# Four operands of three-pass matmuls as two fp16 parts, before as two fp32r parts

## Chip, cores and metric

The kernel runs on one core of one Trainium2 chip. The metric is the device time of one launch in microseconds, the median of several runs. The engines are TensorE (PE, with its weight loads listed apart as PEld), VectorE (DVE), ScalarE (ACT), GpSimd (POOL) and SyncE (SP), which here only issues DMAs.

## What is computed

One transformer layer in fp32 on 2048 tokens of width 128: a layer norm, causal attention with 16 heads of 64, a residual, a second layer norm, and a feed-forward part with one shared and 8 routed experts, of which each token takes two.

```
x = x + attention(layernorm(x), qkv_w, qkv_b, out_w, out_b)
x = x + ffn(layernorm(x), gate_w, expert_gate, expert_up, expert_down, shared_...)

attention:  qkv = einsum('bse,ehd->bshd', x, qkv_w) + qkv_b;  q, k, v = split(qkv)
            logits = einsum('bqhd,bkhd->bhqk', q, k) / sqrt(64), causal mask
            attn = einsum('bhqk,bkhd->bqhd', softmax(logits), v)
            return einsum('bqhd,hde->bqe', attn, out_w) + out_b
```

The change is in two of these products: the projection to q and k, and the output projection of the attention.

## The kernel before

Five instruction streams are written out by hand, one for each engine, and semaphores tie them. The order on each engine is the order of the code. Matrices are held transposed, 128 features on the partitions and the 2048 tokens (T) along the columns, in 4 blocks (NB) of 512 columns (BLK).

**Split operands.** For accuracy close to fp32, an operand is held as two parts, a rounded high part and a low part that holds the rest, and a product of two such operands is three matmuls into the same PSUM bank: high x high, high x low, low x high. Helper `mm3` issues them, at lines L1198, L1199 and L1200. Its users are the two products below. The high parts are made by a converting copy (of ACT for the weights and the first norm, L705, L709, L646; of DVE for the attention output, L1048), the low parts by a subtraction (of POOL for the weights, L544 and L549; of DVE for the norm, L815, and the attention output, L1050). The parts of q and k, of v, of the probabilities and of the routed experts are fp16 already.

**Prologue** (up to some 47 us): the input is normalised and turned into `xn_hi` and `xn_lo`, the weights of the first pair of heads are split, and the four blocks of q and k of head 0 are projected.

**Heads** (some 47 to 720 us): for each of 16 heads PE walks through 20 slots, one for each pair of key tiles of a block of queries (`GROUPS`; block b has 2(b+1) of them). A slot holds the scores (`scores`, L1308 and L1309, two fp16 matmuls for each of two key tiles, up to 512 columns), a causal mask (L1321), and the product of probabilities and v of the slot three before (`p_times_v`, L1340, L1342, L1344: short fp16 matmuls of 64 or 65 columns). ACT takes two exponentials of each slot's scores (L719, L720), POOL subtracts them for the low part of the probabilities (L585).

Between them stand background tasks, which use three PSUM banks (`bg`) in turn: PE writes one, DVE drains it. Their slots are fixed by tables (`V_SLOTS`, `ATT_SLOTS`, `ATT_LAST`) and by a planner that spreads the maxima. They are:

- `qk`, for the next head, in slots 0 to 3: `mm3` of `w_hi`, `w_lo` with `xn_hi`, `xn_lo`, 512 columns; DVE drains it in L1007 and L1009 (ACT's L674 for head 0). SP's queue then copies the parts from one set of partitions to another (L434, L440, L447), and PE waits for them before the first maximum of each four tiles;
- `max`, in slots 4 to 17 or so: the scores once more (L1233, fp16), of which DVE takes row maxima (L1024 with the mask, L1028 without), then `shift` (L1238);
- `v`, two for each head (L1223, plain fp32);
- `att_t` and `att_y`, for a finished pair of heads, in slots 6/8, 10/12, 16/18 of the odd head and 4/6 of the next even one: four transposes (L1243), DVE's split into `att_hi` and `att_lo` (L1048, L1050), then `mm3` of `wo_hi`, `wo_lo` with these, and DVE adds the bank to the residual (L1053). The last pair doesn't use `mm3` but one fp32 matmul (L1249).

So `mm3` is issued 64 times for q and k (4 of them in the prologue) and 28 times for the output.

**The rest** (from some 720 us): second norm, routing, shared expert, a scatter of rows, 39 tiles of the routed experts and the sum of all. No operand of it is among those that change.

## Time and profile before

| | us |
|---|---|
| median of 3 runs | 928.4 |
| lowest and highest run | 926.62, 929.88 |
| the profiled execution, its own time | 927.27 |
| its span in the trace | 925.5 |
| PE, DVE, ACT, POOL busy | 862.5, 696.2, 685.6, 712.2 |
| mean granted TensorE clock, of full speed | 0.979 |

How to read it: the span runs from the first to the last instruction of the program, 1.8 us less than the execution's own time. An engine's busy time is the union of its instructions' times. Matmuls overlap in it: each row of a matmul holds also the time in which its results leave the array, so that what a matmul costs the next one is read from start to start.

### The profile page before, as it was taken

What the parts mean: (1) busy time and instruction counts of PE and PEld (TensorE: products, weight loads), DVE (VectorE), ACT (ScalarE), POOL (GpSimd) and SP (SyncE); (2) the same over time, 40 slices, a digit from 0 to 9 for tenths busy, and PEclk for the clock granted to TensorE, in tenths of its full rate; (3) what the DMA queues carried; (4) which work ended last, traced back from release to release, by engine and by line L of the source; (5) the groups of instructions that cost most, each with busy time, mean ns of one, the idle gap of its engine ahead of it and who ended that gap; (6) DMA issues with size and microseconds to landing.
All of it is one profiled execution on the core that took longest, in us unless ns stands there. A gap on an engine that the chain in (4) does not pass through costs nothing.

```text
span 925.5 us, 25699 instructions
## 1 busy us (share of the span) xinstructions
PE 862.5 (93%) x10266; PEld 595.1 (64%) x10266; DVE 696.2 (75%) x1771; ACT 685.6 (74%) x842; POOL 712.2 (77%) x448
## 2 busy tenths in 40 slices
PE   4788999999999999999999999999999798859996
PEld 3455667666666666666666676666666564438886
DVE  7798797888879797978797979796978356535445
ACT  4456788988898888888988898888889963114442
POOL 1466889998899889988988898888889967344442
PEclk9799999999999999999999999999999999879999
DMA  5121232323232424232301020202020001112214
GB/s 179 24 66 50 56 67 64 67 56 67 63 71 52 75 56 81 59 73 67 66 21 39 19 48 1 57 1 47 2 47 2 2 1 38 46 35 68 61 46 144
DMA packets 60149, 48.33 MB, mean 52 GB/s; under 512 B 8688, under 2 KB 57714, under 8 KB 59904
## 3 DMA queue, kind: packets, MB, share of 16 engines
q1 hardware_dynamic: 57760, 42.48, 20.3%
q0 software_dynamic: 2272, 4.22, 1.3%
q8 instruction: 83, 1.36, 0.6%
q14 instruction: 34, 0.28, 0.1%
HBM read 13.93 MB, written 16.29 MB: 33 GB/s over the span
## 4 chain that ended last, share of the span: by engine, by line
PE 61%; DVE 24%; issue 4%; POOL 4%; ACT 3%; DMA 2%; another core or an unknown queue 1%; SPq 0%; POOLq 0%; DVEq 0%; ACTq 0%
DVE row_max L1028 10%; PE st L1308 7%; PE st L1309 7%; PE bg L1233 6%; PE pv L1340 5%; PE pv L1342 4%; PE pv L1344 4%; POOL p_parts L585 4%; DVE junk L1024 3%; PE bg L1223 3%; PE bg L1483 3%; PE bg L1198 3%; PE bg L1199 2%; PE bg L1200 2%; DVE att_parts L1050 2%
## 5 line engine op out<-in xcount | busy, mean ns | idle before, releaser
L585 POOL TENSOR_TENSOR p_parts<-prob,p_parts 128x1024 f16<-128x1024 f32 x320 | 613.2, 1938 | 101.1 <-ACT p_parts L720 99.0
L719 ACT ACTIVATE prob<-st,p_bias 128x1024 f32<-128x1024 f32 x320 | 330.9, 1034 | 110.5 <-PE st L1309 78.6
L720 ACT ACTIVATE p_parts<-st,p_bias 128x1024 f16<-128x1024 f32 x320 | 330.3, 1032 | 0.0
L1028 DVE TENSOR_REDUCE row_max<-bg 128x1 f32<-128x512 f32 x384 | 250.5, 684 | 8.4 <-PE bg L1233 7.1
L1340 PE MATMUL pv<-v_parts,p_parts 128*128 128x65 f16 x2176 | 232.7, 193 | 3.1 <-POOL p_parts L585 2.6
L1342 PE MATMUL pv<-v_parts,p_parts 128*128 128x64 f16 x2176 | 233.0, 195 | 0.0
L1344 PE MATMUL pv<-v_parts,p_parts 128*128 128x65 f16 x2176 | 232.0, 192 | 0.0
L1308 PE MATMUL st<-qk_parts 128*128 128x512 f16 (+3 forms) x640 | 222.2, 350 | 5.8 <-ACT p_parts L720 3.5
L1340 PEld LDWEIGHTS pv<-v_parts,p_parts 128*128 128x128 f16 x2176 | 202.3, 96 | 28.0 <-DVE attn L1080 8.8
L1309 PE MATMUL st<-qk_parts 66*128 66x512 f16 (+3 forms) x640 | 220.3, 350 | 0.0
L1233 PE MATMUL bg<-qk_parts 128*128 128x512 f16 (+3 forms) x640 | 210.7, 352 | 9.5 <-DVE row_max L1028 2.2
L1342 PEld LDWEIGHTS pv<-v_parts,p_parts 128*128 128x128 f16 x2176 | 201.8, 97 | 16.0 <-issue 0.3
L1344 PEld LDWEIGHTS pv<-v_parts,p_parts 128*128 128x128 f16 x2176 | 202.2, 99 | 0.0
L1024 DVE CUSTOM_DVE_ANT_0 junk<-bg,mask_wide 128x128 bf16<-128x128 f32 (+3 forms) x256 | 121.5, 482 | 3.0 <-PE bg L1233 2.0
L1233 PEld LDWEIGHTS bg<-qk_parts 128*128 128x128 f16 x640 | 62.9, 98 | 76.1 <-DVE row_max L1028 13.2
L1308 PEld LDWEIGHTS st<-qk_parts 128*128 128x128 f16 x640 | 62.7, 98 | 61.5 <-issue 22.5
L1309 PEld LDWEIGHTS st<-qk_parts 66*128 66x128 f16 x640 | 62.6, 98 | 42.5 <-issue 1.1
L1007 DVE TENSOR_SCALAR qk_parts<-bg,qk_bias 128x512 f16<-128x512 f32 x60 | 44.9, 748 | 59.7 <-PE bg L1200 59.7
L622 POOL DMA_INDIRECT y_dram<-p_parts,v_parts x39 | 37.8, 969 | 50.0 <-DVE p_parts L1159 37.4
L777 ACT ACTIVATE prob<-st 128x352 f32<-128x352 f32 x39 | 18.1, 463 | 51.0 <-PE st L1464 41.3
L1167 DVE TENSOR_TENSOR prob<-prob,st 128x352 f32<-128x352 f32 x39 | 20.3, 521 | 46.1 <-issue 40.4
L1009 DVE SCALAR_TENSOR_TENSOR qk_parts<-bg,qk_bias,qk_parts 128x512 f16<-128x512 f32 x64 | 47.9, 751 | 3.4 <-ACT qk_parts L674 1.3
(230 smaller groups left out, 1086.5 us busy)
## 6 DMA issues: line engine op xcount, KB each, us to landing
qk_parts<-qk_parts SPq DMA_DIRECT2D x192, 64.0 KB, 2.0
row_dram<-fill SPq DMA_DIRECT2D x8, 1290.0 KB, 10.3
qk_parts<-qk_parts SPq DMA_DIRECT2D x16, 256.0 KB, 3.0
stage_raw<-ffn_w SPq DMA_DIRECT2D x16, 176.0 KB, 2.6
v_parts<-row_dram SPq DMA_DIRECT2D x39, 64.5 KB
qk_parts<-y_dram SPq DMA_DIRECT2D x8, 256.0 KB, 4.7
w_raw<-qkv_w SPq DMA_DIRECT2D x8, 192.0 KB, 2.3
down_w<-ffn_w SPq DMA_DIRECT2D x1, 1536.0 KB, 8.2
```

What stands on the lines that cost most here:

```text
L585: nc.gpsimd.tensor_tensor(o, a, b, ALU.subtract).then_inc(p_lo_ready, 1)
L719: nc.scalar.activation(o32, src, ACT.Exp, bias=p_bias[:], scale=D ** -0.5)
L720: nc.scalar.activation(o16, src, ACT.Exp, bias=p_bias[:], scale=D ** -0.5).then_inc(exp_done, 1)
L1009: nc.vector.scalar_tensor_tensor(out=q_lo_shift[s][:, blk(b)], in0=bank, scalar=bias, in1=k_lohi[s][:, blk(b)], op0=ALU.add, op1=ALU.subtr ...
L1024: nc.vector.tensor_tensor_reduce(masked[k % BGRING][:, 0:width], bank[:, 0:width], mask_wide[:, BLK - width:BLK], 1.0, -3.0e38, ALU.add, A ...
L1028: nc.vector.tensor_reduce(row_max[:, t, c:c + 1], bank, AX_X, ALU.max).then_inc(bg_drained, 1)
L1233: mm = nc.tensor.matmul(bank[:, 0:width], q_hihi[s][:, tile(t)], k_lohi[s][:, c * BLK:c * BLK + width], start=True, stop=True)
L1308: nc.tensor.matmul(out, k_lohi[s][:, tile(kt)], q_hihi[s][:, q], start=True, stop=False)
L1309: mm = nc.tensor.matmul(out, k_hi_one[s][0:D + 2, tile(kt)], q_lo_shift[s][0:D + 2, q], start=False, stop=not diagonal)
L1340: nc.tensor.matmul(out, p_hi[:, n % PRING, cols], v[:, 0:D + 1], start=(kt == 0 and j == 0), stop=False, skip_group_check=True)
L1342: nc.tensor.matmul(out[:, 0:D], p_hi[:, n % PRING, cols], v[:, D + 1:VW], start=False, stop=False, skip_group_check=True)
L1344: mm = nc.tensor.matmul(out, p_lo[:, n % PRING, cols], v[:, 0:D + 1], start=False, stop=(kt == 4 * b + j), skip_group_check=True)
```

## The change

The types of four groups of buffers change from fp32r (4 bytes) to fp16 (2 bytes): `xn_hi` and `xn_lo` (the normalised input), `split`, which holds `w_hi`, `w_lo` (projection weights) and `wo_hi`, `wo_lo` (output weights), and `att_parts`, which holds `att_hi` and `att_lo`. The streams are not touched: every engine has the same instructions in the same order before and after, with other types of operands. The buffers become smaller, by 8 KB for each partition for the normalised input, 3 KB for `split`, 2 KB for `att_parts`, and what is allocated behind them moves by that.

```diff
-F32, F32R = mybir.dt.float32, mybir.dt.float32r
+F32 = mybir.dt.float32
...
-        att_parts = sb("att_parts", [P, 2 * BLK], F32R)
+        att_parts = sb("att_parts", [P, 2 * BLK], F16)
...
-        xn_hi = sb("xn_hi", [P, T], F32R)
-        xn_lo = sb("xn_lo", [P, T], F32R)
+        xn_hi = sb("xn_hi", [P, T], F16)
+        xn_lo = sb("xn_lo", [P, T], F16)
...
-        split = sb("split", [P, 12, P], F32R)
+        split = sb("split", [P, 12, P], F16)
```

## Rows read from the trace of the kernel before

**Rows 1.** The page: span, then busy us and share of each engine.
```profile
span 925.5 us, 25699 instructions
...
PE 862.5 (93%) x10266; PEld 595.1 (64%) x10266; DVE 696.2 (75%) x1771; ACT 685.6 (74%) x842; POOL 712.2 (77%) x448
```

**Rows 2.** The page: chain that ended last, by engine, then by line.
```profile
PE 61%; DVE 24%; issue 4%; POOL 4%; ACT 3%; DMA 2%; another core or an unknown queue 1%; SPq 0%; POOLq 0%; DVEq 0%; ACTq 0%
DVE row_max L1028 10%; PE st L1308 7%; PE st L1309 7%; PE bg L1233 6%; PE pv L1340 5%; PE pv L1342 4%; PE pv L1344 4%; POOL p_parts L585 4%; DVE junk L1024 3%; PE bg L1223 3%; PE bg L1483 3%; PE bg L1198 3%; PE bg L1199 2%; PE bg L1200 2%; DVE att_parts L1050 2%
```

**Rows 3.** Busy us of a steady stretch: PE, PEld, DVE, ACT, POOL; clock, DMA share, GB/s.
```profile
260.00:360.00 100.00, 99.08 (x1318) 67.68 (x1317) 83.06 (x192) 87.68 (x97) 90.77 (x52) 1.00 0.37 72
```

**Rows 4.** Weight loads: L1198 (ns: min/median/max), L1233 (busy us, mean ns, idle before).
```profile
L1198 PEld LDWEIGHTS bg<-xn_hi,split x64: 186/188/338, 12.1 to 683.1; 128*128 128x128 f32 x64
...
L1233 PEld LDWEIGHTS bg<-qk_parts 128*128 128x128 f16 x640 | 62.9, 98 | 76.1 <-DVE row_max L1028 13.2
```

**Rows 5.** PE in order of time (start us, duration us): an output projection, fp32r.
```profile
301.34 0.19 PE L1344 MATMUL pv<-v_parts,p_parts 128*128 128x65 f16 x1
301.36 0.48 PE L1198 MATMUL bg<-att_parts,split 128*128 128x512 f32 x1
301.68 0.40 PE L1199 MATMUL bg<-att_parts,split 128*128 128x512 f32 x1
...
302.15 0.39 PE L1308 MATMUL st<-qk_parts 128*128 128x512 f16 x1
302.38 0.38 PE L1309 MATMUL st<-qk_parts 66*128 66x512 f16 x1
```

**Rows 6.** PE in order of time: as many columns, all fp16.
```profile
304.85 0.20 PE L1344 MATMUL pv<-v_parts,p_parts 128*128 128x65 f16 x1
304.88 0.38 PE L1233 MATMUL bg<-qk_parts 128*128 128x512 f16 x1
...
305.75 0.38 PE L1308 MATMUL st<-qk_parts 128*128 128x512 f16 x1
```

**Rows 7.** PE in order of time: slot 18, from ahead of L1198 to behind it.
```profile
138.38 0.38 PE L1309 MATMUL st<-qk_parts 66*128 66x512 f16 x1
...
139.46 0.33 PE L1309 MATMUL st<-qk_parts 66*128 66x384 f16 x1
```

**Rows 8.** PE in order of time: the first projection of the prologue.
```profile
12.14 0.78 PE L1198 MATMUL bg<-xn_hi,split 128*128 128x512 f32 x1
12.71 0.63 PE L1199 MATMUL bg<-xn_lo,split 128*128 128x512 f32 x1
13.14 0.63 PE L1200 MATMUL bg<-xn_hi,split 128*128 128x512 f32 x1
```

**Rows 9.** Waits: who waited for whom, us in total, times, longest.
```profile
DVE qk_parts L1007 <- PE bg L1200: 59.7, 44, 3.7
...
DVE res L1053 <- PE bg L1200: 9.0, 22, 0.7
```

**Rows 10.** In order of time, with the idle time before: POOL, then DVE.
```profile
175.03 6.32 POOL L585 TENSOR_TENSOR p_parts<-prob,p_parts 128x1024 f16<-128x1024 f32 x3 [0.94 <-ACT p_parts L720]
...
264.14 2.13 POOL L585 TENSOR_TENSOR p_parts<-prob,p_parts 128x1024 f16<-128x1024 f32 x1 [0.94 <-ACT p_parts L720]
...
239.99 0.69 DVE L1048 CAST att_parts<-bg 128x512 fp32r<-128x512 f32 x1 [0.42 <-PE bg L1243]
```

**Rows 11.** Pieces of the chain in order of time: start us, us, what.
```profile
370.57 2.92 DMA qk_parts<-qk_parts
...
637.37 3.81 DMA qk_parts<-qk_parts
```

**Rows 12.** Groups by line and shape: busy us, mean ns, idle before.
```profile
L1016 DVE CAST v_parts<-bg 128x512 f16<-128x512 f32 x28 | 19.4, 692 | 13.4 <-PE bg L1223 13.2
...
L1048 DVE CAST att_parts<-bg 128x512 fp32r<-128x512 f32 x28 | 19.3, 690 | 3.2 <-PE bg L1243 2.9
...
L544 POOL TENSOR_TENSOR split<-w_raw,split 128x256 fp32r<-128x256 f32 x8 | 5.8, 725 | 5.5 <-ACT split L705 5.5
```

## The prediction

> **What bounds the kernel now.** I read the totals first: one core, a profiled execution of 927.27 us with a span of 925.5 us, PE busy 93% of it and no other engine above 77% [rows 1]. A busy PE says little here, since a matmul row of 0.38 us is followed by the next one after 0.22 us, so I went on to the chain of waits. It gives PE 61% and DVE 24% [rows 2], and it names all three lines of the group of three matmuls that the change touches: L1198 with 3%, L1199 and L1200 with 2% each. The 92 groups of three take about 0.79 us each (301.36 to 302.15 from start to start [rows 5]), 72.7 us or 7.9% of the span; the chain's 3 + 2 + 2% is rounded, and nearly all of that is on the path. Following the chain in order of time, I find 86 of the 92 on it. The six that are not start at 12.1, 17.3, 48.5, 61.0, 369.5 and 636.3 us.
>
> In a stretch of the steady heads PE is busy 99.1 of 100 us at the full clock, POOL 90.8, ACT 87.7, DVE 83.1 [rows 3]. So TensorE sets the pace, with short stretches in which DVE (the row maxima) or POOL (the low parts of the probabilities) ends last.
>
> **The change, part by part.** No instruction is added, dropped or moved on any engine. Four kinds of buffers change type: the normalised input, the split projection weights, the split output weights and the split attention output.
>
> *Weight loads and matmuls.* A stationary part in fp32r loads in 188 ns, one in fp16 (L1233, same 128x128) in 98 ns [rows 4]. What counts is start to start. One group of today: from L1344 at 301.34, the last matmul ahead of it, to L1309 at 302.38 are 1.04 us, for one short matmul and four of 512 columns [rows 5]. The same row of sizes all in fp16: L1344 at 304.85, then L1233 at 304.88, L1308, L1309, L1233 and again L1308 at 305.75, that is 0.90 us, 0.22 for each of 512 columns [rows 6]. The first interval of the fp32r group is 0.32 against 0.22 us (a long load cannot hide behind a 65-column matmul that is over in 0.03 us), the next two are 0.47 together against 0.44, and the fp16 matmul behind the group has 0.23 against 0.22. Difference: **0.14 us for each group**. The streaming rate itself is nearly the same in both types, so this is all that there is.
>
> How many: 64 groups are projections (16 heads, 4 blocks), 28 are output projections (7 pairs, 4 blocks). 81 of them follow a short L1344. 7, those of slot 18, follow L1309 with 512 columns, and there the load is mostly hidden: 138.38 to 139.46 is 1.08 us today [rows 7], against four intervals of 0.22 and one of 384 columns at 0.17, 1.05; gain about 0.04. The 4 of the prologue run at a lower clock: 0.57 us for the first interval, 0.43 for the second [rows 8], gain 0.14 as well.
>
> On the path lie 77 of the 81 (77 x 0.14 = 10.8 us), all 7 (0.3 us) and 2 of the prologue (0.3 us): 11.4 us.
>
> *What is late next.* A shorter group only pays until another engine ends last. Behind the projections DVE stands idle for the result: 44 waits of L1007 on L1200, 59.7 us, 1.4 us each; behind the output projections 22 waits of L1053, 9.0 us, 0.41 us each [rows 9]. All that is well over 0.14. The 16 groups of slot 3 have no such wait, since DVE normalises there, but its next wait on PE comes soon behind and is again longer than 0.14 (0.42 us at 239.99 [rows 10]). POOL's long stretches at the ends of the early even heads start with a wait, too: 0.94 us at 175.03 [rows 10], so they start earlier as PE does. POOL is idle 9.2 us of 100 [rows 3], and a pair of heads (89.1 us from 175.03 to 264.14) wants only 11 x 0.14 = 1.5 us.
>
> One cover is gone already: q and k parts go by SP's queue from one set of partitions to another, and slot 4 needs them. At 370.57 such a copy takes 2.92 us to land and the row maxima of slot 4 wait for it [rows 11]. It is issued behind the group of slot 2 or its drain, so what the group of slot 3 saves is lost there. Two such places are the groups at 369.5 and 636.3, which I have left out already; I charge two more of the fourteen steady heads with the same, by choice, since PE now comes to slot 4 a little earlier against the copy: 2 x 0.14 = 0.3 us back.
>
> *Writing and splitting the parts.* DVE's cast into fp32r takes 690 ns (L1048), its cast of the same size into fp16 takes 692 ns (L1016) [rows 12]: nothing. The low part is a subtraction with a PSUM operand in both, at the same pace. POOL's subtraction for the weights (L544) takes 725 ns for 256 elements, 8 times [rows 12]; no row shows that size in fp16, so I bound it by the same row from both sides, half of it or twice: 8 x 0.36 = 2.9 us of POOL's work less, or 5.8 us more, on an engine with 9 us in 100 to spare. In the whole of the time I take zero, with POOL's stretch at the end of a head (rival B) as the place where more would show. ACT's copies into fp16 are not on the path in the steady heads. The DMAs are the same, the four buffers are never a source or a target of one.
>
> Sum: 11.4 - 0.3 = **11.1 us** less, 927.27 - 11.1 = 916.2 us against the profiled execution. The median of the runs shown, 928.4, lies 1.1 us above that execution, so I forecast **917.3 us**.
>
> The Trainium skill speaks against the larger part of this. Its page "TensorE: Matmul & The Clock Gate", section "Weight-path perf modes", says of 8-bit operands that a weight load scales with the number of columns, not with bytes; the same section also says that a fast load applies to 128 weights of any type but FP32. By the first sentence the load would stay as long as it is; by the second it gets shorter. The trace sides with the second for fp16 against fp32r (98 and 188 ns), and I follow the trace.
>
> **The rivals.**
>
> *A, forecast.* 9.5 to 12.5 us less, 916 to 919.
>
> *B, another engine swallows part of it.* The place would be POOL's stretches at the ends of four even heads, where the 5 groups of such a head would then give nothing (4 x 5 x 0.14 = 2.8 us), and the SP copies ahead of slot 4 in all heads from 2 on (12 more groups, 1.7 us). Together 11.1 - 4.5 = 6.6 us less, 921.8. For it: POOL at 90.8% and two copies that bind today. Against it: the waits of rows 9 and 10, which are all longer than the gain.
>
> *C, the load does not get shorter*, so the change does not do what it should. Then the first interval stays at 0.32 and only the small terms are left: (0.47 - 0.44) + (0.23 - 0.22), some 0.04 us for each of the 86 groups, 3.4 us less, 925.0. For it: today's fp16 loads are all of other buffers. Against it: the load of L1233 takes 98 ns whatever stands ahead of it, and in [rows 6] it follows a short matmul without a delay. This is also what the skill's sentence on columns would give.
>
> *D, slower.* The copies of the q and k parts collide with other transfers or with each other. Their landing today takes 2.0 us in the median and 2.92 and 3.81 us in the two places where they bind [rows 11]. If PE's earlier arrival at slot 4 meets copies that land as late as 3.81 us in each of the 14 steady heads, each head pays up to 1.8 us, less the margin that it has. It decides from 11.1 / 14 = 0.8 us a head; at 1.0 us a head the change ends at 928.4 + 2.9 = 931.3. For it: those two places, without a plain reason for the slow landing. Against it: size, number and order of the copies stay, and their source, DVE's drain of the group, moves forward with PE, so the margin shrinks by one group's 0.14 us at most.
>
> **How the numbers follow.** A 0.76, B 0.11, C 0.05, D 0.04, and 0.04 for what I have not seen. Most likely 917.3. The range: below, all 92 groups on the path give 12.9 us (915.5), and a quick chip some 1.5 us more, as the runs shown spread from 926.6 to 929.9; so 914.2. Above, it takes B in: 922.0. Outside lie C, D and the unseen, and the edges. A measurement of this kernel tells some 0.3% (2.8 us) from no change. A, B and C are faster by more than that, C only just, so faster 0.90, within 0.3% 0.05, slower 0.05.
>
> **What the changed profile would show.** L1198 to L1200 as f16, with a load of 98 ns; L1344 to L1309 across a group 0.90 us in place of 1.04; 64 us in place of 73 for the 92 groups; the pair of heads, 89.1 us long (175.03 to 264.14 for the same POOL stretch), shorter by 1.5 us; DVE's waits for L1200 shorter in sum, not gone. L1048, L1050 as long as now. If B holds, the groups are shorter and the waits of POOL's or DVE's successors on PE grow: PE idle before L1340 for POOL, or before L1233 for a DMA. If C holds, the load row reads 188 ns in fp16. The forecast is wrong if the intervals shrink but the pair of heads does not, or if the tail behind 720 us, which holds none of the groups, changes length by more than 1 us.

## Result and the profile after

| us | before | after |
|---|---|---|
| median of 4 runs each (lowest to highest) | 928.47 (926.62 to 929.88) | 919.51 (917.31 to 920.30) |
| ratio, with 95% interval | | 0.990 (0.988 to 0.992) |
| profiled execution, its span | 927.27, 925.5 | 918.86, 917.1 |
| mean granted TensorE clock, of full speed | 0.979 | 0.974 |

The change makes the kernel 9.0 us faster; 11.1 were forecast, and the time lies 2.2 us above the forecast of 917.3 and inside its range. A second pair, with more runs of each (below), gives 10.5 us. The direction, the place and the mechanism of the forecast held. What was off are small terms: the loss to late copies was sized too small, the prologue gave nothing, and the part behind the last group, taken as fixed, came out 2 us longer in both pairs of profiles.

The page of the kernel after: span, busy times, and the chain that ended last, by engine and by line (answers to [rows 1, 2]):

```profile
span 917.1 us, 25699 instructions
...
PE 853.2 (93%) x10266; PEld 577.4 (63%) x10266; DVE 695.6 (76%) x1771; ACT 684.9 (75%) x842; POOL 710.7 (77%) x448
...
PE 60%; DVE 25%; issue 5%; POOL 4%; ACT 3%; DMA 2%; SPq 1%; POOLq 0%; DVEq 0%; ACTq 0%
DVE row_max L1028 10%; PE st L1308 7%; PE st L1309 7%; PE bg L1233 7%; PE pv L1340 5%; PE pv L1342 4%; PE pv L1344 4%; POOL p_parts L585 4%; DVE junk L1024 3%; PE bg L1483 3%; PE bg L1223 3%; PE bg L1200 2%; PE bg L1198 2%; PE bg L1199 2%; DVE att_parts L1050 2%
```

The instructions are as many as before, PE's busy time falls by 9.3 us, and L1198 goes from 3% to 2% of the chain. VectorE, ScalarE and GpSimd keep their busy times to 1.5 us.

The weight loads of L1198 after (ns: min/median/max, as in [rows 4]):

```profile
L1198 PEld LDWEIGHTS bg<-xn_hi,split x64: 95/96/151, 12.1 to 672.9; 128*128 128x128 f16 x64
```

PE in order of time, an output projection after (start us, duration us), the counterpart of [rows 5]:

```profile
297.92 0.19 PE L1344 MATMUL pv<-v_parts,p_parts 128*128 128x65 f16 x1
297.95 0.38 PE L1198 MATMUL bg<-att_parts,split 128*128 128x512 f16 x1
298.16 0.38 PE L1199 MATMUL bg<-att_parts,split 128*128 128x512 f16 x1
298.38 0.38 PE L1200 MATMUL bg<-att_parts,split 128*128 128x512 f16 x1
298.60 0.38 PE L1308 MATMUL st<-qk_parts 128*128 128x512 f16 x1
298.81 0.38 PE L1309 MATMUL st<-qk_parts 66*128 66x512 f16 x1
```

The load is 96 ns where it was 188. From L1344 to L1309 are now 0.89 us, where [rows 5] had 1.04, and every interval is 0.21 or 0.22, the first one too. Over the 81 groups behind a short L1344 the median is 892 ns, and it was 1039 ns before. Taken apart by the width of the L1308 that follows, the difference is 0.150 us for 66 of them and 0.147 us for the other 15; I use **0.148 us for each group**.

The steady stretch after, columns as in [rows 3]:

```profile
260.00:360.00 100.00, 98.75 (x1348) 66.36 (x1346) 81.81 (x191) 90.15 (x101) 92.17 (x53) 1.00 0.35 66
```

TensorE is as full as before, and ScalarE and GpSimd are 2.5 and 1.4 points busier, since their work comes in less time. TensorE still sets the pace.

Waits after (who waited for whom: us in total, times, longest), against [rows 9]:

```profile
DVE qk_parts L1007 <- PE bg L1200: 53.6, 43, 3.5
...
DVE res L1053 <- PE bg L1200: 6.7, 22, 0.6
```

In order of time, GpSimd and then VectorE, against [rows 10]:

```profile
173.92 2.13 POOL L585 TENSOR_TENSOR p_parts<-prob,p_parts 128x1024 f16<-128x1024 f32 x1 [0.94 <-ACT p_parts L720]
...
261.42 2.13 POOL L585 TENSOR_TENSOR p_parts<-prob,p_parts 128x1024 f16<-128x1024 f32 x1 [0.94 <-ACT p_parts L720]
...
237.41 0.69 DVE L1048 CAST att_parts<-bg 128x512 f16<-128x512 f32 x1 [0.25 <-PE bg L1243]
```

Groups after, against [rows 12], the second one by its line alone (ns: min/median/max):

```profile
L1048 DVE CAST att_parts<-bg 128x512 f16<-128x512 f32 x28 | 19.3, 690 | 2.0 <-PE bg L1243 1.8
...
L544 POOL TENSOR_TENSOR split<-w_raw,split x8: 667/671/686, 9.2 to 594.6; 128x256 f16<-128x256 f32 x8
```

VectorE's waits for the group became shorter and did not go, so VectorE did not become what ends last behind these groups. The pair of heads between the two stretches of GpSimd takes 87.50 us, and it took 89.11: 1.6 us less, 1.5 were forecast. GpSimd still begins its long stretch behind the same wait of 0.94 us. The cast takes 690 ns in both types, and GpSimd's subtraction 671 ns against 725.

### The profile page after: what moved, and what is told of

Its sections match the earlier page's. It is cut to its first block, busy times and chain, and to the rows that moved or that the text cites. A ratio compares the mean times of both kernels' runs of the same rounds, so it can differ in the third digit from the quotient of the medians.

```text
span 917.1 us, 25699 instructions
## 1 busy us (share of the span) xinstructions
PE 853.2 (93%) x10266; PEld 577.4 (63%) x10266; DVE 695.6 (76%) x1771; ACT 684.9 (75%) x842; POOL 710.7 (77%) x448
## 4 chain that ended last, share of the span: by engine, by line
PE 60%; DVE 25%; issue 5%; POOL 4%; ACT 3%; DMA 2%; SPq 1%; POOLq 0%; DVEq 0%; ACTq 0%
DVE row_max L1028 10%; PE st L1308 7%; PE st L1309 7%; PE bg L1233 7%; PE pv L1340 5%; PE pv L1342 4%; PE pv L1344 4%; POOL p_parts L585 4%; DVE junk L1024 3%; PE bg L1483 3%; PE bg L1223 3%; PE bg L1200 2%; PE bg L1198 2%; PE bg L1199 2%; DVE att_parts L1050 2%
## 5 line engine op out<-in xcount | busy, mean ns | idle before, releaser
L585 POOL TENSOR_TENSOR p_parts<-prob,p_parts 128x1024 f16<-128x1024 f32 x320 | 612.4, 1935 | 93.5 <-ACT p_parts L720 91.6
L1340 PE MATMUL pv<-v_parts,p_parts 128*128 128x65 f16 x2176 | 232.7, 193 | 3.2 <-POOL p_parts L585 2.6
L1344 PE MATMUL pv<-v_parts,p_parts 128*128 128x65 f16 x2176 | 231.9, 192 | 0.0
L1308 PE MATMUL st<-qk_parts 128*128 128x512 f16 (+3 forms) x640 | 221.7, 349 | 7.4 <-ACT p_parts L720 4.6
L1309 PE MATMUL st<-qk_parts 66*128 66x512 f16 (+3 forms) x640 | 220.6, 351 | 0.0
L1340 PEld LDWEIGHTS pv<-v_parts,p_parts 128*128 128x128 f16 x2176 | 202.3, 96 | 28.4 <-DVE attn L1080 9.0
L1233 PE MATMUL bg<-qk_parts 128*128 128x512 f16 (+3 forms) x640 | 210.7, 353 | 9.8 <-DVE row_max L1028 2.1
L1344 PEld LDWEIGHTS pv<-v_parts,p_parts 128*128 128x128 f16 x2176 | 202.2, 99 | 0.0
L1024 DVE CUSTOM_DVE_ANT_0 junk<-bg,mask_wide 128x128 bf16<-128x128 f32 (+3 forms) x256 | 121.7, 483 | 3.1 <-PE bg L1233 2.1
L1233 PEld LDWEIGHTS bg<-qk_parts 128*128 128x128 f16 x640 | 62.9, 98 | 77.4 <-DVE row_max L1028 13.1
L1309 PEld LDWEIGHTS st<-qk_parts 66*128 66x128 f16 x640 | 62.4, 97 | 52.6 <-issue 1.4
L1308 PEld LDWEIGHTS st<-qk_parts 128*128 128x128 f16 x640 | 62.9, 98 | 50.0 <-ACT p_parts L720 7.0
L1007 DVE TENSOR_SCALAR qk_parts<-bg,qk_bias 128x512 f16<-128x512 f32 x60 | 44.9, 749 | 53.8 <-PE bg L1200 53.6
```

What stands on the lines that cost most here:

```text
L585: nc.gpsimd.tensor_tensor(o, a, b, ALU.subtract).then_inc(p_lo_ready, 1)
L1024: nc.vector.tensor_tensor_reduce(masked[k % BGRING][:, 0:width], bank[:, 0:width], mask_wide[:, BLK - width:BLK], 1.0, -3.0e38, ALU.add, A ...
L1233: mm = nc.tensor.matmul(bank[:, 0:width], q_hihi[s][:, tile(t)], k_lohi[s][:, c * BLK:c * BLK + width], start=True, stop=True)
L1308: nc.tensor.matmul(out, k_lohi[s][:, tile(kt)], q_hihi[s][:, q], start=True, stop=False)
L1309: mm = nc.tensor.matmul(out, k_hi_one[s][0:D + 2, tile(kt)], q_lo_shift[s][0:D + 2, q], start=False, stop=not diagonal)
L1340: nc.tensor.matmul(out, p_hi[:, n % PRING, cols], v[:, 0:D + 1], start=(kt == 0 and j == 0), stop=False, skip_group_check=True)
```

## The experiments

To compare parts of a run, I cut it at the starts of the `shift` drain (L1040), one for each head: h to h+1 is the stretch between those of heads h and h+1. The drain for head h comes in slot 18 of head h-1, so that h to h+1 is in the main the time of head h. Head 15 itself comes behind its drain; the last scores of the kernel before (L1308) start at 764.2 us and the last L1340 at 769.1, so the heads end near 770 us and not near 720, as I had put it at the start. In the table "once more" are repeats of the unchanged kernels; stretches that repeat a pattern are left out.

| us | before once more | after once more | q, k only | output only | 4 matmuls | 2 matmuls |
|---|---|---|---|---|---|---|
| 1 to 2 | 45.77 | 45.20 | 45.02 | 44.98 | 45.54 | 44.54 |
| 2 to 3 | 43.42 | 42.64 | 42.84 | 43.22 | 44.76 | 41.37 |
| 3 to 4 | 45.67 | 44.85 | 45.14 | 45.38 | 46.08 | 44.26 |
| 6 to 7 | 43.43 | 42.63 | 42.84 | 43.21 | 43.93 | 41.37 |
| 7 to 8 | 45.68 | 45.32 | 46.24 | 45.79 | 46.08 | 44.11 |
| 9 to 10 | 45.68 | 45.10 | 45.42 | 45.50 | 46.07 | 44.24 |
| 10 to 11 | 43.43 | 42.63 | 42.84 | 43.24 | 43.94 | 41.37 |
| 13 to 14 | 45.89 | 45.46 | 45.19 | 45.54 | 45.40 | 43.97 |
| start of head 15's | 713.94 | 703.42 | 706.25 | 712.12 | 720.06 | 692.21 |

A stretch that starts with an even head is called short here (43.4 us before), one that starts with an odd head long (45.7 us). The expectations below go by the head at the end of a stretch: their odd stretches are the short ones, their even ones the long ones. The three chips on which the experiments ran give the kernel before other times (929.0, 908.8 and 908.5 us; the last section comes to that), so each is compared on its own chip.

### Both kernels once more, and one half of the change at a time

My theory: the whole gain is the weight load, so it splits by the number of groups, 64 for q and k, 28 for the output. The rival was that something else in one of the two halves carries it, or takes it back.

> The kernel before once more, unchanged. It gives a second profile of it. The changed kernel gained 8.4 us of span in the first pair of profiles: 10.05 us up to the start of the last pair's output projection (L1249), of which 1.0 us had been given back in head 0, and then 1.7 us given back behind it, where none of the changed matmuls is. Theory (the granted clock of TensorE, at its low level in other places of the prologue and of the routing from one execution to the next, by chance): this second profile differs from the first by 0.5 to 2.5 us in the stretches 0 to 60 us and 770 to 830 us, by less than 0.5 us in the heads 2 to 15 altogether apart from a single hiccup, and its ratio is 1.000 within 0.002. Rival (the faster heads shift the phase in the same way each time): the second profile of before shows its low clock in the same places as the first, to 0.3 us.

> The changed kernel once more, unchanged. Clock by chance: its stretches 0 to 60 us and 770 us to the end differ from those of the first profile of it by 0.5 to 2.5 us, and the 13 stretches from head to head (h2 to h15) are the same within 0.1 us each. Ratio to before 0.988 to 0.991 (9 to 11 us less). Rival (the losses outside the heads belong to the change): head 0 costs 1.0 us more than before again, and the tail 1.7 us more.

The first half alone has `xn_hi`, `xn_lo` and the projection weights in fp16:

```diff
-        split = sb("split", [P, 12, P], F32R)
+        split = sb("split", [P, 8, P], F16)
+        wo_split = sb("wo_split", [P, 4, P], F32R)
```

> Only the normalised input and the projection weights are fp16; the output weights, in a tensor of their own, and the attention output stay fp32r. 64 of the 92 groups are fast. A group counts at its measured 0.148 us: 60 groups in the heads x 0.148 = 8.9 us, less some 1.5 us for those of slot 3 or of head 0 that are not on the path: 7.4 us less, ratio 0.992, and 4 x 0.148 = 0.6 us less for each head. If the output projections were what counted (rival): under 3 us.

The second half alone has `att_parts` and the output weights in fp16:

```diff
-        split = sb("split", [P, 12, P], F32R)
+        split = sb("split", [P, 8, P], F32R)
+        wo_split = sb("wo_split", [P, 4, P], F16)
```

> Only the attention output and the output weights are fp16; projections stay fp32r. 28 groups: 21 x 0.148 + 7 x 0.05 = 3.5 us less, ratio 0.9963, and together with the kernel with only the projections in fp16 the same as the whole change within 1 us. If gains of the two kinds cover each other (rival), the sum of both alone is 1.5 us or more above the whole.

| | median us | ratio to before, 95% | gain us |
|---|---|---|---|
| before once more | 929.05 | 1.000 (0.998 to 1.002) | 0.0 |
| after once more | 918.54 | 0.989 (0.987 to 0.991) | 10.5 |
| q and k only | 921.59 | 0.993 (0.990 to 0.995) | 7.4 |
| output only | 925.54 | 0.996 (0.995 to 0.998) | 3.5 |

The two halves give 10.9 together, the whole 10.5. The profiles agree: from the start of head 1's drain to head 15's the whole saves 9.9 us, the first half 6.8 and the second 3.5.

Of the two repeats, the kernel before took the same time again, and its clock fell in other places (its low stretch in the prologue began at 29.8 us, not at 30.6), as I had expected. Of the changed kernel two expectations failed. Four of the stretches, not none, differ from the first profile by more than 0.1 us: 1 to 2 by 0.40, 7 to 8 by 0.23, 9 to 10 by 0.32, 13 to 14 by 0.26. And the loss in the tail came again, as the rival said: behind head 15's drain the two profiles of before take 209.98 and 211.22 us, the two of after 212.03 and 213.09. The loss in head 0 did not come again.

How the gain splits over single stretches shows in the starts of the `shift` drain, heads 9 to 11. The rows give ns (min/median/max of the drain), then first and last start in us. Before once more:

```profile
L1040 DVE SCALAR_TENSOR_TENSOR shift_row<-bg,shift_row x3: 278/278/279, 405.4 to 494.5; 16x128 f16<-16x128 f32 x3
```

After once more:

```profile
L1040 DVE SCALAR_TENSOR_TENSOR shift_row<-bg,shift_row x3: 278/278/278, 399.9 to 487.7; 16x128 f16<-16x128 f32 x3
```

With q and k alone (one more line stands above it, so that it is L1041 here and in the next):

```profile
L1041 DVE SCALAR_TENSOR_TENSOR shift_row<-bg,shift_row x3: 278/278/279, 401.6 to 489.8; 16x128 f16<-16x128 f32 x3
```

With the output alone:

```profile
L1041 DVE SCALAR_TENSOR_TENSOR shift_row<-bg,shift_row x3: 278/278/278, 405.2 to 494.0; 16x128 f16<-16x128 f32 x3
```

First to last start is 89.1, 87.8, 88.2 and 88.8 us. In the table, a short stretch has five groups behind a short matmul and one of slot 18: 5 x 0.148 + 0.06 = 0.80 us (0.06 is the difference of the medians over the 7 groups of slot 18, 1.087 and 1.028), and 43.43 - 42.63 is 0.80. With q and k alone it is four groups, 0.59, measured 0.59; with the output alone 0.148 + 0.06 = 0.21, measured 0.20 (0.19 to 0.22). In a long stretch the six groups should give 0.89, and give 0.82 where nothing else happens (3 to 4); with the output alone it is 0.30 there, as two groups should, with q and k alone 0.53, not 0.59, so the missing 0.07 belongs to q and k. One stretch went the wrong way: 7 to 8 takes 46.24 us with q and k alone, 0.56 more than before, since a copy comes late there (below). So the shorter groups explain the short stretches to 0.01 us, the long ones to 0.07 us. The rival falls: neither half carries the gain alone, and neither takes it back.

### Is it the load that stood out? A longer matmul ahead of it

A 188 ns load can hide behind a matmul of 512 columns (0.22 us), but not behind one of 65. If the gain is the exposed load, it must shrink when the background task stands behind a score pair. If fp32r matmuls themselves were the slow part, it would stay.

```diff
-                    first, second_at = (0, 0) if h == H - 1 else (1, 2)
+                    first, second_at = (0, 0) if h == H - 1 else (0, 1)
```

In the new order, with the types of before and with those of after:

> The kernel before with the first background task of each slot of heads 0 to 14 issued on TensorE behind the slot's first pair of score matmuls, not ahead of it. The fp32r groups of slots 0 to 3 then follow an L1309 of 128 to 512 columns, no longer a 65-column L1344. Theory (0.10 of the 0.148 us is a weight load that a short matmul cannot hide): groups behind a 512-column matmul cost as those of slot 18 do, 0.05 us more than fp16; the span from the matmul ahead of the group to the one behind is 0.05 us over the fp16 kernel with the same order. So this order narrows the gap between the two types from 0.80 us to 0.3 us a head. What the new order does by itself, to both kernels, I can't tell: between 5 us less and 10 us more, since scores come earlier and the maxima later. Rival (the first interval is long for another reason, a change of type from fp16 to fp32r): the gap stays at 0.8 us a head.

> The same new order in the changed kernel. Theory of the hidden load: it is only 3 to 6 us faster than the kernel before in the same order (10.5 us in the old order). Rival: 9 to 11 us faster.

Measured: 942.65 us (ratio 1.036, 1.034 to 1.038) and 938.00 (1.032, 1.030 to 1.035) against 908.83 for the kernel before on that chip. Between them are 4.65 us, where the old order has 10.5 on the first chip and 11.7 on the third. PE in order of time, in the new order with the types of before:

```profile
382.68 0.38 PE L1309 MATMUL st<-qk_parts 66*128 66x512 f16 x1
382.71 0.58 PE L1198 MATMUL bg<-xn_hi,split 128*128 128x512 f32 x1
383.13 0.40 PE L1199 MATMUL bg<-xn_lo,split 128*128 128x512 f32 x1
383.37 0.40 PE L1200 MATMUL bg<-xn_hi,split 128*128 128x512 f32 x1
383.60 0.34 PE L1308 MATMUL st<-qk_parts 128*128 128x384 f16 x1
```

The same with the types of after:

```profile
382.24 0.38 PE L1309 MATMUL st<-qk_parts 66*128 66x512 f16 x1
382.45 0.38 PE L1198 MATMUL bg<-xn_hi,split 128*128 128x512 f16 x1
...
383.10 0.38 PE L1308 MATMUL st<-qk_parts 128*128 128x512 f16 x1
```

From L1309 to L1308 are 0.92 and 0.86 us. The same step, from the matmul ahead of the group to the first one behind it, has these medians: 922 and 868 ns over the 66 groups behind 512 columns, 815 and 762 ns over the 15 behind 256 columns, 867 and 813 ns over the 7 behind 384; behind the 65 columns of the old order it is 814 and 676 ns. So the difference of types is 0.054 us in all 88 groups of the new order and was 0.138. Some 0.08 us of a group was the load that stood out behind the short matmul, and it is hidden behind 256 columns already. The rest stays with fp32r: 0.054 us in this step, mostly in the intervals of 0.24 and 0.23 against 0.22, and 0.065 with the next matmul, 88 x 0.065 = 5.7 us in all, of which 4.65 reach the end. The theory holds: the change from fp16 to fp32r between L1309 and L1198 is there in the new order too, so it isn't what made the first interval long. The new order by itself is far worse, by 34 us with the types of before, where I had expected at most 10: PE is busy only 96.5 of 100 us between 260 and 360 us and waits for ScalarE (1.16 us ahead of the L1308 at 382.47). I did not follow that further.

### One matmul less and one more in each group

How much of a shorter group reaches the end? Two kernels of after's types change the group by a whole matmul of 0.216 us, 92 x 0.216 = 19.9 us of PE's time. The first leaves out L1199:

```diff
-                nc.tensor.matmul(out, w_hi_ap, x_lo_ap, start=False, stop=False, skip_group_check=skip)
```

> The changed kernel without the second matmul of each group of three (high weights by the low part of the moving operand, L1199): 92 fp16 matmuls of 512 columns less, 0.216 us each, so TensorE has 19.9 us less work. It tells how much more there is before another engine ends last. Theory (each stretch has the covers seen in the waits: DVE 0.36 us ahead of L1007 in slot 2, none in slot 3, 0.3 us ahead of L1053, and the copies of slots 3 and 4): the first 0.15 us of a group paid nearly in full, the next 0.22 pays in part: odd stretches 42.63 to 41.8, all in all 12 to 16 us less than the changed kernel. Rival (TensorE alone bounds): 18 to 19 us less.

The second adds low x low:

```diff
+                nc.tensor.matmul(out, w_lo_ap, x_lo_ap, start=False, stop=False, skip_group_check=skip)
```

> The changed kernel with a fourth matmul in each group (low weights by low moving part, which the sum of two parts would need in full): 92 fp16 matmuls of 512 columns more, 0.216 us each. It asks the same as the kernel with two matmuls from the other side. There TensorE's 0.216 us a group came back in full in the odd stretches (42.63 to 41.37) and by half or less in the even ones. Theory (going up, TensorE is what ends last, more and more): odd stretches 42.63 + 6 x 0.216 = 43.93 us, even ones 44.86 + 1.30 = 46.16, together 17 to 20 us slower than the changed kernel. Rival (covers work both ways, half of it hides in waits for DVE): 8 to 12 us slower.

With four the time is 913.07 us (before on that chip 908.49, ratio 1.005, 1.003 to 1.007), 16.3 more than after there (896.82, below), where 17 to 20 were expected. With two it is 885.58 (before 908.83, ratio 0.974, 0.972 to 0.976), 11.2 less than after, where 12 to 16 were expected. Both lie just outside, on the side of less effect. After itself did not run on the chip of the kernel with two, so I use 896.82 of the other quick chip, where before takes 0.3 us less. (The starts of head 15's drain give the same: 720.06, 703.55 and 692.21 us, steps of 16.5 and 11.3.)

| step | PE work us | time us | passed through |
|---|---|---|---|
| four matmuls to three | 19.9 | 16.3 | 82% |
| fp32r to fp16, three matmuls | 13.0 (12.4 in the heads, 4 x 0.148 in the prologue) | 10.5 | 81% |
| three matmuls to two | 19.9 | 11.2 | 57% |

Most short stretches give a whole matmul for each of their six groups both ways (43.94 to 42.63, 41.37; 6 x 0.216 = 1.30). With four matmuls 2 to 3 (44.76) and 12 to 13 (44.31) are longer than that. With two matmuls three short stretches fall short: 4 to 5 takes 43.03 and 8 to 9 takes 42.06, and 14 to 15 takes 40.68 where after has 40.86. The other four take 41.37. In the long ones TensorE's wait for GpSimd (L585) grows from 0.25 to some 0.54 us in 3 to 4, 5 to 6, 7 to 8 and 9 to 10, and copies bind in five stretches. So a shorter group paid less the second time than the first. The steady stretch with two matmuls, columns as in [rows 3]:

```profile
260.00:360.00 100.00, 98.15 (x1368) 66.38 (x1367) 82.79 (x190) 91.24 (x103) 95.03 (x55) 1.00 0.30 63
```

GpSimd is at 95% there.

### Copies that land late

In the long stretches 1 to 2, 7 to 8, 9 to 10 and 13 to 14 the gain is 0.57, 0.36, 0.58 and 0.43 us instead of 0.82, together 1.34 us less. In the first two TensorE waits for a copy of the parts of q and k. Pieces of the chain in order of time in after (start us, us, what):

```profile
363.88 0.76 DVE qk_parts L1007
...
364.66 0.54 SPq L434
...
365.24 0.60 SPq L434
...
365.94 3.22 DMA qk_parts<-qk_parts
...
369.30 0.38 PE bg L1233
```

The copy of the second block for head 8 lands after 3.22 us, where the median of all is 2.0, and PE waits for it. In 9 to 10 the view names another wait of PE (L1233 on `row_max` L1024, 0.51 us at 457.33), but that task waits for the same kind of copy too, and one (L440) landed at 457.20: it was issued late, behind copies that took 2.5 to 3.1 us.

In 13 to 14 it is a copy of another kind. SP in order of time, then PE, in after:

```profile
619.42 1.18 SPq L471 DMA_DIRECT2D qk_parts<-shift_row  x2
...
623.07 0.38 PE L1308 MATMUL st<-qk_parts 128*128 128x512 f16 x1 [0.93 <-issue]
```

The first L1308 of a head waits in the code for the two 4 KB copies of `shift_row` (L1299), whose landing the profile doesn't hold, so the view can name nothing. Their packets tell: they end 1.77 us after the second issue here (at 620.01), and after 1.40 us in most heads.

Why do some land late? I counted over the 208 copies of q and k in the trace of after: of the 62 that take over 2.3 us, 50 have a packet of one of the two queues that the profile calls instruction (q8 and q14) in their time, of the 146 quick ones 20. In before it is 47 of 59 and 17 of 149. Sixteen of the 62 are the 256 KB copies (L447), which take 3.0 us in the median and never under 2.9; without them it is 41 of 46 in after and 37 of 43 in before. That is a correlation; the cause wants a run. I take these queues to bring the engines' code, q8 in 83 packets of 16 KB over the span; no row says what is in a packet. Two rivals: that the collision depends on how many instructions PE has behind it (then extra matmuls in the prologue move it to other heads), or that it is the addresses of the smaller buffers.

> The changed kernel with 64 small matmuls (128x32, ident by ident, into the bank that the attention uses later) at the start of TensorE's stream, where it waits some 9 us for the first norm. They cost no time there but move all later instructions of TensorE by 128 places. In the profiles of the changed kernel the copies of q and k of heads 2, 8, 10 and 14 land in 2.5 to 3.6 us where 1.9 to 2.0 is usual, each time beside one of the 16 KB transfers of the instruction queue, which come every 10 us or so, and heads 7 and 9 (in which the copies for 8 and 10 are made) save 0.3 to 0.5 us where head 11 saves 0.8. Theory (these transfers delay the copies, and at a fixed place of the program): the stretches from head to head that are slow move to other heads: 7 to 8 or 9 to 10 falls to 44.9 us from 45.3 to 45.5, and some other even stretch (5 to 6, 11 to 12, 3 to 4) rises by 0.3 us or more. Total within 1.5 us of the changed kernel. Rival (something else of heads 7 and 9, such as the fills of row_dram): the stretches stay as they are, to 0.1 us.

```diff
+            for _ in range(64):
+                nc.tensor.matmul(pv[:, 0:32], ident[:], ident[:, 0:32], start=True, stop=True)
```

This one, with the lines ahead of the first transposes of the prologue, was built badly. `ident` is fp32, and each such matmul stands as two rows. The group of the added line in its trace (busy us, mean ns | idle before):

```profile
L1351 PE MATMUL pv<-ident 128*128 128x32 f32 x128 | 27.5, 401 | 1.6 <-POOL ident L524 1.6
```

There are 255 instructions more, and the instruction queue has 84 packets in place of 83. If those 255 fill nearly one packet, the pattern was moved round by a whole period. The time is 915.96 us (ratio 1.007, 1.006 to 1.009), with the 27 us of work partly beside the start; the long stretches 7 to 8 and 9 to 10 stay as in after, 45.74 and 45.40 against 45.55 and 45.42. By the letter of the expectation the rival had this run (and the total missed its 1.5 us by far). But if it was moved by a whole period, both rivals say the same here. So again with fp16 operands, 64 loads and 64 matmuls in the same place, ahead of the first transposes of the prologue, together with after unchanged and with after whose buffers are padded to the old addresses:

> The changed kernel once more, unchanged, as the reference beside the next three and as a pair with the kernel before on this chip. The kernel before took 909 us on the chip of the last four runs and 929 us on the first, with the difference in the routing and the first expert tiles (some 760 to 820 us), where none of the changed matmuls is. Theory (the gain is made in the heads, so it is the same number of microseconds on any chip): 9 to 11.5 us less than before, odd stretches from head to head 42.63 us and even ones 44.86, to 0.03.

The extra matmuls with fp16 operands:

```diff
+            ident_h = ident[:].bitcast(F16)
+            for _ in range(64):
+                nc.tensor.matmul(pv[:, 0:32], ident_h[:, 0:P], ident_h[:, 0:32], start=True, stop=True)
```

> The changed kernel with 64 fp16 matmuls (the bits of ident read as fp16, 32 columns) at the start of TensorE's stream. The last try put in 64 fp32 matmuls, each of which ran as two with two loads: 255 instructions, almost exactly one 16 KB transfer of the instruction queue, so that these transfers stood in the same places of the program, and the slow stretches with them; and they took 27 us, 19 of them on the path. These are 128 instructions, half a transfer, and some 0.11 us each, 7 us, inside TensorE's 9 us of waiting. Theory (instruction transfers delay the copies of q and k): the stretches 7 to 8 (45.3 to 45.7 us so far) and 9 to 10 (45.1 to 45.4) come down to 44.9, the transfers now fall in the middle between the old places, and other stretches may rise by 0.3 to 0.5. Rival (something else of these heads): 7 to 8 and 9 to 10 stay above 45.2. Total within 1.5 us of the changed kernel.

The padding:

```diff
         att_parts = sb("att_parts", [P, 2 * BLK], F16)
+        sb("pad0", [P, 2 * BLK], F16)
...
         xn_hi = sb("xn_hi", [P, T], F16)
+        sb("pad1", [P, T], F16)
         xn_lo = sb("xn_lo", [P, T], F16)
+        sb("pad2", [P, T], F16)
...
         split = sb("split", [P, 12, P], F16)
+        sb("pad3", [P, 12, P], F16)
```

> The changed kernel with unused buffers behind the four changed ones, so that every buffer lies at its old address. Theory (types alone matter): same as the changed kernel, ratio to it 1.000 within 0.0015, stretches the same to 0.03 us. Rival (part of the gain is from where the buffers lie): more than 1.5 us slower.

| us | after, third time | extra matmuls | padded |
|---|---|---|---|
| median | 896.82 | 898.76 | 898.17 |
| ratio to before, 95% | 0.989 (0.985 to 0.992) | 0.989 (0.987 to 0.991) | 0.988 (0.986 to 0.990) |
| 1 to 2 | 45.38 | 44.11 | 45.47 |
| 3 to 4 | 44.87 | 45.27 | 44.86 |
| 5 to 6 | 44.88 | 45.14 | 44.87 |
| 6 to 7 | 43.03 | 43.32 | 42.63 |
| 7 to 8 | 45.61 | 44.87 | 45.27 |
| 9 to 10 | 44.99 | 44.88 | 45.39 |
| 11 to 12 | 44.20 | 44.70 | 44.20 |
| 13 to 14 | 45.21 | 44.22 | 44.84 |

After for the third time gains 11.7 us against before on that chip, just over the 9 to 11.5 expected; 1 to 2, 6 to 7, 7 to 8, 9 to 10, 11 to 12 and 13 to 14 are not the 42.63 or 44.86 forecast. With the extra matmuls the loss moves: 1 to 2, 7 to 8 and 13 to 14 fall by 0.7 to 1.3 us, 3 to 4, 5 to 6, 6 to 7 and 11 to 12 rise by 0.3 to 0.5. The two that the theory named, 7 to 8 and 9 to 10, take 44.87 and 44.88 where 44.9 was forecast, though 9 to 10 stood at 44.99 already. With the padding the loss stays in 1 to 2, 7 to 8 and 9 to 10, 13 to 14 is 0.4 lower, and none of the four others rises. Its median is 1.35 us higher, close to the 1.5 at which the addresses would have counted, but that is no loss in the heads: from head 0's last drain (L1040; L1044 here) to head 15's it takes 638.2 us against 638.8, and its low clock in the prologue lasts 3.4 us longer. So I find no effect of the addresses, and one of the number of instructions ahead. The queues in the time of that copy, in after, 365.9 to 369.2 us (packets, MB, share of 16 engines):

```profile
q1 hardware_dynamic: 343, 0.29, 36.8%
q8 instruction: 1, 0.02, 2.2%
```

and with the extra matmuls, 364.8 to 366.8 us, where the view has no row of an instruction queue:

```profile
q1 hardware_dynamic: 258, 0.22, 44.9%
```

There the same copy lands after 1.94 us (issued at 364.82, landed at 366.76), and the chain has no DMA in it (start us, us, what):

```profile
366.80 0.17 PE st L1309
366.97 0.18 PE bg L1233
367.17 0.56 DVE junk L1024
```

The other stretches fit, in this one profile. In 13 to 14 the packets of `shift_row` now end after 1.40 us, and the wait of 0.9 us ahead of L1308 is gone. In 3 to 4 and 6 to 7, which rose, they end after 1.95 and 2.16 us, each time with a 16 KB packet of q8 beside them, and L1308 waits 0.33 and 0.53 us. In 5 to 6 and 11 to 12 two copies of q and k have such a packet beside them (2.7 to 3.0 us), push the next ones back, and L1233 waits 0.41 and 0.47 us.

This shows, by a change that leaves the heads as they are and puts 128 instructions of TensorE, 2 us of work, into the wait at the start, that the transfers of the instruction queue decide in which heads PE waits, and that with one a copy can land more than 1 us later. Moving them does not make a faster kernel: head 15's drain starts at 703.55 us without and 702.27 with the extra matmuls, and the medians, 896.82 and 898.76, lie within each other's spread (1.9 us apart, where at most 1.5 was expected). Of the kernels that form the full sum of three matmuls, none beats after measurably.

## Why the prediction was right, and where it was off

The chain, the count and the mechanism were right, and the time lies in the range. It lies 2.2 us above the most likely value. The two "once more" traces allow an account of the 10.5 us up to head 15's drain (713.94 - 703.42):

| term | forecast us | measured us |
|---|---|---|
| 81 groups behind a short matmul | 81 x 0.14 = 11.3 | 81 x 0.148 = 12.0 |
| 7 groups of slot 18 | 0.3 | 7 x 0.06 = 0.4 |
| prologue, up to the third start of L1040 | 0.3 | -0.2 |
| what groups of the heads do not give (forecast: 4 off the path, 2 behind copies) | -0.8 | -2.2 |
| 0 to 1, which holds no group | 0 | 0.5 |
| sum | 11.1 | 10.5 |

**The rate.** The 0.14 us was read as 1.04 - 0.90 from two single places with two decimals. Over all groups it is 0.148. That is 0.7 us of gain that I had not counted. A median would have been the better row.

**Hidden loads in slot 18.** 0.04 forecast, 0.06 measured (1.03 against 1.09 us), and the new order gives 0.065 for 88 groups.

**The copies are the mis-sized term.** The step "I charge two more of the fourteen steady heads with the same, by choice" was wrong in two ways. It took the loss for one group's 0.14 us at a place, but a stretch in which a copy binds loses 0.24 to 0.46 us. And it took the two places of [rows 11] for fixed ones, while they wander with the transfers of the instruction queue. Four stretches lose 1.34 us, 0.39 of them (13 to 14) by the copies of `shift_row`, for which the forecast had no term. The seven long ones lose 0.07 each besides (0.5 together, a cause that I did not find), and the four groups of head 0, ahead of 0 to 1, give 0.28 of 0.59 us: 2.2 in all. Against it the forecast charged 0.84. This is rival B's copy half, with 1.3 of its 1.7 us, of which some 0.9 by copies of q and k. Its other half, GpSimd at the ends of even heads, does not show: the pair of heads gives 1.6 us. With groups shorter still it would show, as the kernel with two matmuls tells.

**The start.** The prologue has 0.3 us in the forecast and -0.2 in this pair; from one execution to the next it varies more than that (the third start of L1040 is at 46.88 and 46.26 us in the two traces of before). Against it stands 0.5 us that belongs to no group: in 0 to 1 PE waits 0.85 us for a copy of `shift_row` in place of 1.39. In the first pair it was 1.56 in place of 1.34, and with the types of after it is 0.85 or 0.86 in four of the later profiles; why the copy comes earlier there is open. That the sum comes so close to 11.1 owes something to this term, which the forecast did not have: that part is luck.

**Marks.** The load of 98 ns (96), 0.90 us for a group (0.89), the 1.5 us of a pair of heads (1.6), and the waits all came. The lower end of the range has a slip: 915.5 - 1.5 is 914.0, not 914.2. One mark had a slip of the pen: 92 groups would fall from 73 to 72.7 - 92 x 0.14 = 59.8 us, not 64; measured are 0.65 from L1198 to L1308 (297.95 to 298.60), so 60. Another mark failed by its own words: the end behind head 15's drain, without any of the groups, grew from 209.98 to 212.03 us, over the 1 us that I had set. In the second pair it grew again, from 211.22 to 213.09, and the halves have 212.91 and 213.53. So on this chip both pairs of profiles give back some 2 us there, and the spans differ by 8.4 and 8.7 us where the heads had won 10.4 and 10.5. The forecast had nothing for it. It is not the types by themselves: on the quick chips, where the stands of TensorE told of in the last section are missing, the end takes 191.79 us with the types of before (in the new order) and 191.26 with those of after. On the first chip the clock is at its lower level for 20.5 us between 770 and 835 us in both traces of before, and for 24 to 27 us in the four with fp16 parts; why it falls there for longer when the heads end earlier, no run shows. Why the medians give 9.0 us in one set of runs and 10.5 in the other, the profiles don't tell.

**Rivals C and D.** C (a load as long as before) is excluded by the 96 ns. D (slower by late copies) had the right mechanism, but its price for each head was far too high: the copies' landing stays at 2.0 us in the median, and four heads give back 0.24 to 0.46 us, where D needed 1.0 us in each of fourteen. It had no plain reason for the two slow landings; in both places of [rows 11] a 16 KB packet of q8 stands beside the copy.

The rule of the Trainium skill, page "TensorE: Matmul & The Clock Gate", section "Weight-path perf modes", that a load scales with columns and not with bytes, is not what the trace shows for fp32r against fp16: 128 columns take 188 ns in the one and 96 in the other. (The page's sentence speaks of 8-bit operands, and the carrying-over was the prediction's.) Its sentence that a fast load applies to 128 weights of any type but FP32 agrees, if fp32r counts as FP32.

## What to carry to other kernels

Look at the matmul ahead of a weight load: a load costs only what outlasts that matmul, so fp32r cost a group of three 0.148 us behind a matmul of 65 columns and some 0.06 behind one of 256 or 512. Count groups on the chain one by one, take a median interval over all of them, and charge what is waited for (here copies between partitions) by its spread of landing times, not by the places at which it happened to bind in one trace. In this kernel about four fifths of the saved work reached the end, and less the next time. Where the profile calls a wait "issue", look in the code for a copy whose landing it doesn't hold.

## What the hardware did that I had not expected

**Transfers of the instruction queue delay copies.** A 64 KB copy between partitions landed after 1.94 us without and 3.22 us with one in its time, and the packets of a 4 KB copy ended after 1.40 and 1.77 to 2.16 us, as shown above.

**Chips differ in one place.** The kernel before takes 929.0 us on one chip and 908.8 and 908.5 on two others. Up to head 15's drain there is little between them (after once more 703.42 us, after the third time 703.55). Behind it after takes 212.0 us on the first and 191.4 on the third chip, and 17.5 of these 20.6 us are between 760 and 820 us. Columns as in [rows 3]; the same part of the program in after on the first chip:

```profile
762.20:779.00 16.80, 12.69 (x39) 6.04 (x37) 8.43 (x31) 3.47 (x7) 12.84 (x14) 0.98 0.16 52
779.00:808.30 29.30, 27.95 (x76) 13.77 (x76) 16.04 (x70) 6.09 (x12) 9.89 (x11) 0.78 0.16 44
808.30:815.10 6.80, 1.36 (x8) 0.67 (x7) 0.03 (x1) 0.46 (x1) 5.15 (x6) 0.81 0.15 49
```

and in after on the third chip:

```profile
761.30:772.10 10.80, 10.80 (x33) 5.15 (x31) 8.19 (x30) 3.63 (x8) 8.32 (x9) 1.00 0.16 50
772.10:796.00 23.90, 23.38 (x84) 11.64 (x82) 16.06 (x71) 6.02 (x12) 14.44 (x15) 1.00 0.26 67
796.00:796.70 0.70, 0.70 (x6) 0.42 (x5) 0.02 (x1) 0.48 (x2) 0.40 (x2) 1.00 0.00 0
```

That is 52.9 against 35.4 us. Pieces of the chain of after on the first chip, in order of time, show what fills it:

```profile
771.44 0.86 PE pv L1398 x2
...
774.89 4.87 issue
779.76 3.75 PE pv L1398 x4
...
808.26 6.81 issue
```

TensorE stands for 4.87 and 6.81 us and waits for nothing that the profile shows. Behind the first of these the granted clock is 0.78 in the mean of the stretch (so part of it at 1.2 and part at 2.4 GHz), and matmuls of L1398 take 0.94 us each (3.75 / 4) where they take 0.43 ahead of it (0.86 / 2). What holds TensorE there I could not find, and no kernel was built for it; before once more takes as long in the same three parts (16.8, 29.0 and 6.9 us against 16.8, 29.3 and 6.8). In the first profile of before the first stand is 3.52 us, so it is not the same in every execution.

**A low clock by chance in the prologue.** From 40.5 to 46 us the granted clock is 0.69 in after (columns as in [rows 3]):

```profile
40.50:46.00 5.50, 4.90 (x28) 2.13 (x29) 2.75 (x6) 4.26 (x6) 3.59 (x3) 0.69 0.00 0
```

and 1.00 in after once more, the same program:

```profile
40.50:46.00 5.50, 3.76 (x36) 2.15 (x37) 3.69 (x9) 5.30 (x8) 4.15 (x3) 1.00 0.00 0
```

The stretch that holds it takes 12.2 us in the one and 10.7 in the other. The same program shows both, so the types don't decide it (12.1 in the output half and the padded kernel too), and a single execution of this kernel can be 1.5 us longer there by that alone.
